# Second layer of a two-layer graph network: fixed blocks of 2176 edges, transposed sums, and the output computed inside the edge loop

## What is computed

```python
def _directional_msg(x, src, dst, edge_attr, req, W1, b1, W2, b2, n_nodes):
    m = jnp.concatenate([x[src], edge_attr, req_e], axis=-1)      # 128 + 16 + 16
    h = jax.nn.relu(m @ W1 + b1) @ W2 + b2
    return jax.ops.segment_sum(h, dst, num_segments=n_nodes)

h_in  = _directional_msg(x, first half of the edges,  ..., W1f, b1f, W2f, b2f)
h_out = _directional_msg(x, second half of the edges, ..., W1b, b1b, W2b, b2b)
h = (1.0 + eps) * x + h_in + h_out
x = _layernorm(x + relu(h @ Wu + bu))
```

## Time and profile before

| | us |
|---|---|
| median of 3 runs (lowest, highest) | 3563.51 (3556.25, 3569.98) |
| the profiled execution | 3566.67 |
| its span, first to last instruction | 3564.8 |
| projections and layer 0's edge loop | 1743.8 |
| dense passes | 237.4 |
| layer 1, edge loop | 1378.4 |
| layer 1, last part | 205.1 |

### The profile page before, as it was taken

The page is one execution under the profiler, slowest core; times in us unless marked ns, Lnnn a source line. Parts: engine busy times, 40 slices in busy tenths (PEclk is TensorE's granted clock), DMA queues, the critical chain, the costliest instruction groups (busy, mean ns, idle before and its releaser), DMA issues. The chain is left out here.

```text
span 3564.8 us, 40489 instructions
## 1 busy us (share of the span) xinstructions
PE 1972.8 (55%) x9710; PEld 1453.6 (41%) x9711; DVE 1518.9 (43%) x3784; ACT 579.1 (16%) x1373; POOL 1789.5 (50%) x1781
## 2 busy tenths in 40 slices
PE   1525555555555555555577455566556456566687
PEld 1414444444444444444465233334333333334455
DVE  2624444455454454455598323333323233233222
ACT  1401111111111111111133111111111111111121
POOL 1136666566666566556211465556566555656300
PEclk9756666666666666666699566555556565555556
DMA  4322222222222222222011122222222222222500
GB/s 129 102 56 77 76 76 76 72 76 75 75 75 74 74 74 76 73 75 75 21 31 36 45 49 47 47 47 48 47 47 48 46 46 46 49 46 49 28 18 18
DMA packets 229894, 208.88 MB, mean 59 GB/s; under 512 B 152706, under 2 KB 188552, under 8 KB 229741
## 3 DMA queue, kind: packets, MB, share of 16 engines
q0 software_dynamic: 68448, 168.14, 17.9%
q1 hardware_dynamic: 157850, 39.16, 5.2%
q10 hardware_dynamic: 3574, 1.33, 0.2%
HBM read 190.35 MB, written 24.52 MB: 60 GB/s over the span
## 5 line engine op out<-in xcount | busy, mean ns | idle before, releaser
L522 POOL DMA_INDIRECT arena<-kv_tab,arena x850 | 906.8, 1067 | 629.6 <-DMA arena<-i 366.0
L570 POOL DMA_INDIRECT arena<-y_tab,arena x864 | 820.1, 949 | 569.2 <-issue 263.5
L1004 PE MATMUL ps<-w1blk,arena 65*128 x432 | 401.6, 1029 | 284.2 <-ACT arena L762 160.2
L877 PE MATMUL ps<-arena 128*128 x2550 | 273.6, 279 | 454.9 <-ACT arena L673 330.5
L1383 DVE TENSOR_TENSOR arena<-ps,arena 128x512 f32<-128x512 f32 x216 | 149.2, 691 | 877.4 <-remote 512.3
L1010 PEld LDWEIGHTS ps<-arena 128*128 128x128 f32 x1728 | 371.5, 301 | 297.0 <-issue 182.6
L877 PEld LDWEIGHTS ps<-arena 128*128 128x128 bf16 x2550 | 226.0, 127 | 514.4 <-ACT arena L673 354.3
L1010 PE MATMUL ps<-arena 128*128 128x129 f32 x1728 | 379.1, 391 | 72.2 <-ACT arena L765 52.0
L867 PE MATMUL ps<-ident,arena 128*128 128x128 f32 x850 | 216.7, 409 | 311.5 <-DVE arena L1211 305.9
L867 PEld LDWEIGHTS ps<-ident,arena 128*128 128x128 f32 x850 | 147.6, 209 | 360.4 <-DVE arena L1211 314.8
L1377 DVE TENSOR_SCALAR arena<-iota_row,arena,nj 128x128 f32<-128x128 f32 x864 | 244.4, 357 | 22.6 <-issue 14.7
(11 more groups left out here) (238 smaller groups left out, 2170.0 us busy)
## 6 DMA issues: line engine op xcount, KB each, us to landing
arena<-y_tab,arena POOLq DMA_INDIRECT x864
arena<-kv_tab,arena POOLq DMA_INDIRECT x850
arena<-ea SPq DMA_DIRECT2D x216, 32.0 KB
ea<-in_edge_attr_dram SPq DMA_DIRECT2D x2, 3125.0 KB, 22.3
kv_tab<-arena SPq DMA_DIRECT2D x10, 625.0 KB
y_tab<-arena SPq DMA_DIRECT2D x20, 312.5 KB
arena<-i SPq DMA_DIRECT2D x216, 2.0 KB
arena<-d SPq DMA_DIRECT2D x216, 2.0 KB
```

The lines of the kernel that those rows point to most:

```text
L522: g.indirect_dma_start(kv_s[:, u, t, :], None, kv_tab, bass.IndirectOffsetOnAxis(ap=v3(idx, 2)[:, u, t:t + 1], axis=0)).then_inc(l_g[u][k] ...
L570: g.indirect_dma_start(yg_s[:, u, t, :], None, y_tab, bass.IndirectOffsetOnAxis(ap=v3(idx1, U)[:, u, t:t + 1], axis=0)).then_inc(m_g[u], 16)
L877: last = mm(bank(x_)[:, t * D:(t + 1) * D], st_s[:, x_, t * P:(t + 1) * P], qsp[:, ds(tile + part * D, D)], start=(part == 0), stop=(part ...
L1004: mm(bank(1 + (u - 1) % 2), v3(eaT, 2)[0:G * EA + 1, (u - 1) % 2, :], w1blk[:, ds(way, CH)]).then_inc(m_u, 1)
```

## The change

Layer 1 is written anew; the rest is touched only where it hands over.

- **Blocks.** Each half of the edges is cut into 23 fixed blocks of 2176 edges (17 columns of 128), 46 in all, without regard to tiles. A block's sums go to a span of W = 160 nodes that begins at the block's first node; `chunk_table(1)` gives a block as many entries as spans of 160 nodes are needed from its first node to the next block's.
- **Buffers.** Two blocks are in flight instead of six chunks. The gathers of a block go to `yg` in place, in pieces of 6, 6 and 5, and the hidden values and the relu are written there too. A slot is free for new gathers when the block's message sums are through (`m_agg`).
- **Transposed sums.** The gathered rows are now the weight operand and the one-hot of 160 nodes the moving one, so the sums come out as features by nodes. The edge counts come from a reduction of the one-hot on DVE (`hsum`) and a small product.
- **Attributes.** Turned in three pieces of 96 rows per block, and multiplied by a block-diagonal weight of 97 rows, 384 (once 256) columns at a time.
- **Output in the loop.** While block c is worked on, the span of block c-1 is finished: four products of 160 columns, relu, residual, two transposes, layer norm, and a store of 160 rows. Overlapping nodes are stored again by the next block. The last part is gone.
- **The dense passes** copy the turned x (L576) instead of x into `xs`; POOL zeroes `acc1` and the counts at the start of these passes, where DVE zeroed `acc1` at their end.

```diff
+            def gather_edges(u):
+                pool.wait_ge(m_buf, 4)
+                pool.wait_ge(m_ix[u], landed)
+                pool.wait_ge(m_agg, slot_free)
+                for k, (s0, n) in enumerate(PIECES):
+                    for t in range(s0, s0 + n):
+                        g.indirect_dma_start(yg_s[:, u, t, :], None, y_tab, ...).then_inc(m_g[u][k], 16)
```

```diff
+            def pe_msgs(u, new, old):
+                w = 1 - u
+                if new is not None:
+                    way = pe.value_load(...)
+                    attr(u, 0, way)
+                    attr(u, 1, way)
+                    attr(u, 2, way)
+                    pe.wait_ge(m_hot, now)
+                    pe.wait_ge(m_sel, now)
+                    mm(bank(4 + u)[0:2, W:2 * W], v3(sel, 2)[:, u, :], v3(hsum, 2)[:, u, :])
+                    messages(u, 0)
+                    attr(u, 3, way)
+                if old is not None:
+                    base = pe.value_load(...)
+                    pe.wait_ge(m_acc, last_)
+                    to = bank(6)[:, 0:W]
+                    mm(to, w2u[:, 0:D], acc1[:, ds(base, W)], start=True, stop=False)
...
+                    mm(to, dbu[:, :], deg[0:2, ds(base, W)], start=False, stop=True).then_inc(f_o, 1)
+                if new is not None:
+                    attr(u, 4, way)
+                    messages(u, 1)
+                if old is not None:
+                    pe.wait_ge(f_x, last_)
+                    for h in range(2):
+                        last = tp(bank(7)[0:W2, h * D:(h + 1) * D], outT[:, h * W2:(h + 1) * W2], ident[:, :])
+                    last.then_inc(f_tp, 1)
+                if new is not None:
+                    attr(u, 5, way)
+                    attr_T(w)
+                    messages(u, 2).then_inc(m_agg, 1)
```

```diff
+            def dve_hot(u, made_):
+                dve.wait_ge(m_ld[u], landed_)
+                dve.wait_ge(m_dcr, made_)
+                link(tt(hot1_s[:, u, :, :], iota_w[:, None, :].to_broadcast([P, G0, W]), dcr1[:, :, None].to_broadcast([P, G0, W]),
+                        ALU.is_equal))
+                v.tensor_reduce(v3(hsum, 2)[:, u, :], hot1_s[:, u, :, :].rearrange("p g n -> p n g"), AX_X, ALU.add).then_inc(m_hot, 1)
...
+            def dve_msgs(u, new, old):
...
+                if new is not None:
+                    hidden_rows(u, 4)
+                if old is not None:
+                    dve.wait_ge(f_tp, last_)
+                    for h in range(2):
+                        done = v.bn_stats(norm3[0][0:W2, h * 6:(h + 1) * 6], bank(7)[0:W2, h * D:(h + 1) * D])
...
+                if new is not None:
+                    dve_hot(w, now)
+                if old is not None:
+                    dve.wait_ge(f_sd, last_)
+                    dve.wait_ge(f_dma, stored)
+                    link(v.reciprocal(norm3[3][0:W2], norm3[2][0:W2]))
...
+                    done.then_inc(f_out, 1)
+                if new is not None:
+                    hidden_rows(u, 5)
```

More of the change, by code:

```diff
@@ new lines, in attr, with messages @@
+            def attr(u, j, way):
+                s0, n = PIECES[j // 2]
+                a0 = 3 * (j % 2)
+                cols = (min(n, a0 + 3) - a0) * D
+                if j == 0:
+                    pe.wait_ge(m_eT, now)
+                pe.wait_ge(m_hid, block_)
+                mm(bank(j % 3)[:, 0:cols], eaT_s[:, u, (j // 2) * P:(j // 2 + 1) * P], w1blk[:, ds(way + a0 * D, cols)]).then_inc(m_u, 1)
+                pe.reg_add(block_, block_, 1)
+            def messages(u, k):
+                s0, n = PIECES[k]
+                pe.wait_ge(m_con, piece_)
+                for t in range(s0, s0 + n):
+                    last = mm(bank(4 + u)[:, 0:W], yg_s[:, u, t, :], hot1_s[:, u, t, :], start=(t == 0), stop=(t == G0 - 1))
+                pe.reg_add(piece_, piece_, 1)
+                return last
@@ L1164, in chunk_table @@
+                link(ts(below, which, float(nv), float(2 * E), ALU.is_ge, ALU.mult))
                 link(tt(off, off, below, ALU.add))
                 link(ts(off, off, float(end), None, ALU.min))
[L1166 to L1170 removed]
```

652 lines of the change are left out of this document (349 added, 303 removed).

## The result

| | before | after | ratio, 95% interval |
|---|---|---|---|
| median of 4 runs each, us | 3564.67 | 3767.30 | 1.0561 (1.0536 to 1.0586) |
| the same two kernels on chip 0 | 3515.4 | 3686.2 | 1.0492 (1.0445 to 1.0540) |
| the same two kernels on chip 1 | 2966.5 | 2780.4 | 0.9366 (0.9344 to 0.9387) |

The forecast of 3235 us was wrong by 532 us, and the changed kernel was slower. One of the eight executions of the kernel before on chip 0 took 4655 us, for no known reason, and is left out of the ratio.

The account below looks back on a forecast made before the run. The old loop was taken as bound by a ring of waits among SP, POOL and PE. The new span, 2031 + 45 x 26.8 = 3237 us, plus 1.9 minus 3.2, gave 3235 us; 8-in-10 range 3110 to 3450.

Parts of the forecast that it names:

- Hop 0.2: Handoff from PE's transposes of the old block to DVE's statistics in each block: taken as 0.2 us.
- DVE's stretch: DVE's work per block from the transposes' handoff through statistics, one-hot, reduction and normalisation to hidden rows 5: 8.2 us.
- The slower rival: PE's wait for DVE between transposes and hidden rows 5 makes the kernel slower, from 34.1 us per block; chance 0.06.
- P: Time per block in the new layer-1 loop, forecast at 26.8 us.
- No surcharge: DVE's one-hot reduction, reading 640 bytes apart, was given no extra time for the distance: 2.98 us for 2720 elements.
- The rival: The strided reduction on DVE costs double, 3.0 us more per block: P = 29.8, 3371 us; chance 0.09.
- The sum of the chain: PE, DVE and ACT parts following one another per block: 31.6 us at PE's lower clock, 22.2 at full clock.
- a mixed clock: PE runs part of each block at the lower clock, the rest at full: chain 25.7 us, 26.8 with late rises.
- the first rival: Gathers become the bound, PE at full clock nearly throughout: 3101 us; P below 25 had chance 0.20.
- 17 x 1.25 + 2.5 = 23.8 us: POOL's time per block: 17 gathers of 1.25 us, plus 2.5 us for the gather held up by DVE's one-hot.
- Start and end: Around the loop: first gather at 1981 us, 36 us to the first block's sums, 14 us after the last block.
- Its likeliest case: Time per block in the new loop between 25 and 29 us, giving 3155 to 3335 us; chance 0.50.

Follow-up runs that it names:

- the one-hot early: Changed kernel with the next block's one-hot and reduction moved right behind hidden rows 3, ahead of the waits for the old block: 3407.07 us, ratio to before 0.9637 (chip 6).

## Why the prediction was wrong

- **The failed step** is the "Hop 0.2" at the head of DVE's stretch: that DVE sees PE's transposes 0.2 us after they are done. It holds on chips 1 and 15 and fails by 6.3 to 14.2 us, 10.7 in the median, in 43 of the 46 blocks of the profiled run (all that have a burst beside the transposes). The period there is 0.8 us from the last messages to the first gather, 20.9 of gathers, 3.3 until the increment shows, 9.6 of DVE's stretch, 0.8 of relu and 3.1 of messages: 38.5. PE's path from the first attribute product to the transposes, on which the sum stood, is no part of it. By the difference of the two chips late increments make some 650 of the 3767 us.
- **The reason could have been read.** The earlier trace rows hold "remote 22.7" and "remote 47.4" as releasers of L1220, and the waits of before had 512 us of it ahead of L1383. I took "remote" as a gap of the record. In the changed loop one such handoff has 13.5 us of work in a chain behind it. That the ring of six chunks had less behind its own is my reading of why it lost less; no run shows it.
- **The slower rival** named the right place (PE waiting for DVE's stretch between the transposes and hidden rows 5) and the right deciding point, P = 34.1, but with another price, the reduction's. (Its 5.5 us are 2.0 ns per element, not 1.9.) It got 0.06.
- **The reduction** was mis-sized: 4.70 us, not 2.98. "No surcharge" rested on 40 elements; at 2720 it is 1.72 us. Without it the 2.98 were right: read side by side it takes 2.986 us. The rival had the right mechanism with 3.0 us. The Trainium skill (Advanced Engine Details and Errata, SBUF Cachelines) says that accesses each on another line pay a penalty; the trace agrees, 1.57 times.
- **The sum of the chain** at full clock was 22.2 us; with 1.7 for the stride it is 23.9, the measured period on chip 1. Its parts were nearly right: PE 13.4 us where 13.1 were reckoned, DVE 9.6 against 9.9, relu 0.8 against 0.95. But the forecast stood on a mixed clock, and that step was too slow as well. From the end of the last messages to the transposes it counts 4.8 + 7.2 + 1.6 = 13.6 us; on chip 1 PE took 10.4. The mean clock over the loop is 0.78 on chip 1, within the 0.7 to 0.8 foretold, and 0.67 in the profiled run, against 0.58 before. This is the first rival, P below 25.
- **POOL**: 17 x 1.25 + 2.5 = 23.8 us, measured 23.9 on chip 1. The gather beside the one-hot took 3.62 us instead of 0.94, 2.7 more. Gathers beside the reduction took 0.95: the Trainium skill's rule (SBUF — State Buffer, Who interferes with whom) that tensor_reduce never contends holds here.
- **Start and end**: the first gather at 1991 instead of 1981, the first block's sums 37 us later (foretold 36; on chip 1, 38), but POOL sees their increment only 45 us after that gather, and the second block takes 55.6 us. From the last messages to the end it is 9.7 us, foretold 14. There were 46 blocks, as foretold.
- **With chip 1's start and period** the working gives 1654 + 50 + 45 x 23.9 = 2780 us; measured 2780. To the microsecond this is luck: the start took 2 us more, the second block 2 more, the end 4 less. The forecast's ratio, 3235 / 3564 = 0.908 (range 0.873 to 0.968), would have held the 0.9366 there. That would have been luck in part too: 329 us of gain were foretold and 186 measured, and the loop, foretold to go from 1378 to 1242 us, did not get shorter there by the estimate above. Its likeliest case, P of 25 to 29, held on no chip.

## What to carry to other kernels

Look at who releases a wait, not only at how long it is: a large "remote" between two engines of one core, with the releasing instruction long done, can be a property of the handoff, and it may then be paid again by each chain that is built on one. Where POOL gathers in long bursts, keep what PE signals off the path that sets the period: give its readers other work in front, or let the burst wait for the signal. Before a run is read, make sure that its edit is in the trace: register additions that nothing reads were not there. And measure a kernel beside its rival on more than one chip before its order is believed.

## What the hardware showed that I had not expected

- While POOL's indirect gathers follow each other every 1.25 us, increments that PE makes can show up to 14 us late at DVE, ACT and POOL in the changed kernel's bursts of 17 and up to 20 us in one of 34, and come in clumps within 0.15 us; those of DVE and ACT do not. They mostly show 2.3 us after the end of a burst of 12, 2.4 after 13, 3.0 to 3.3 after 17 (2 with the one-hot early) and 4.7 after 34; after the 51 gathers at the start of the first trace it was 6.0. Some get through in the midst of a burst. As many transfers of the same size started by SP do nothing of the kind.
- It depends on the chip: chips 0, 3 and 6 (and the one of the first times) show it, 1 and 15 (twice) do not, and the same kernel runs 3515 to 3565 or 2955 to 2966 us. The Trainium skill (Perfetto Trace Analysis, Tensor Engine Instruction (MATMUL, LD_WEIGHTS)) has PE's increment sent by PSUM once all is written, unlike DVE's. That would set PE apart from the others, as seen; that this is the way on which it is held was not tried, and why chips differ is open.
- Not shown: whether "late in the trace" is wholly "late at the reader". The readers' starts agree with it each time that I looked.
- Three memsets of one column fit into the gap between two gathers at 0.02 us. Two memsets of 160 columns in a chain took the pitch from 1.25 to 2.03 us.
